# Moving the squares of queries and keys from GpSimd to ScalarE in a fused decoder's first self-attention

## Chip, cores and metric

The kernel runs on one core of a Trainium2 chip, as one launch. The metric is device time in microseconds (us); lower is better. TensorE is called PE here, its weight loads PEld, VectorE DVE, ScalarE ACT and GpSimd POOL.

## What is computed

Two decoder layers on x of shape (16, 128, 256), float32. Each layer is a self-attention, a cross-attention and a feed-forward part, each followed by a residual addition and a layer norm. The change is in the first part of layer 0, which treats the 16 batch entries as 16 separate tiles of 128 tokens with 16 heads of 128:

```
q  = rope(rmsnorm(x @ Wq  + bq,  qn_w))        # rmsnorm: t * rsqrt(mean(t*t) + eps) * w
lk = rope(rmsnorm(x @ Wlk + blk, kn_w))
lv = x @ Wlv + blv
ck, cv = keys and values of 32 compressed entries (weighted sums of 4 tokens)
sparse = softmax over the 8 largest of q.ck, times cv
local  = softmax(causal q.lk), times lv
x = layernorm(x + ((sparse + local) / 2) @ Wo + bo)
```

The mean of squares of every head of q and lk is what the changed instructions feed.

## The kernel before, in words

`l0_attention` gives each engine its own program. The programs meet only through semaphores. A `Count` is a semaphore with a fixed number of increments in each tile; `of(b, k)` is its value after the k-th of tile b, and `before(c, b, k, n)` the value n increments ahead of that.

The order of the work is written out by hand: the list `order` names pieces with a lag, and `pipeline` emits on every engine, in that order, the pieces which that engine has. In pass i a piece with lag 0 works on tile i, one with lag 1 on tile i-1. So a pass mixes the projections of tile i with the attention of tile i-1. Passes 0 and 1 are emitted apart, passes 2 to 15 are a loop, and two passes drain it. The list holds

```
... ("s1", 1), ("norm1", 2), ("q", 0), ("sparse_exp", 1), ("sparse_prob", 1), ("rot_q", 0), ("norm2", 2),
("e0", 1), ("k", 0), ("e1", 1), ("turn_sparse", 1), ("m0", 1), ("sum_q", 0), ("top2", 1), ("entries", 0), ("m1", 1) ...
```

What each engine does in the pieces that matter here:

- Piece `q`, and likewise `k`: PE projects 4 chunks of 512 columns (L452, L454) into two PSUM banks in turn; ACT copies each chunk to `raw` (L605); before the change POOL then squares the whole 128x2048 of it into `sq` (L388). There is one `sq` tile for both. So the keys' square waits until DVE has summed the queries' (`summed`, L387).
- Piece `rot_q` (DVE): rotary embedding of the raw queries, L702 to L707. Piece `sum_q` (DVE): sums of squares of each head, L748, and a scale, L749; the keys have `rot_k` and `sum_k`.
- Pieces `sum_q`, `k_norm`, `comp_kv` on POOL: the powers -1/2 (L394, L399, L408), and the scaling of the rotated keys (L403).
- Pieces `e0` and `e1` (ACT): exponentials of the local scores of head groups 0 and 1, L645, with the bias `a_nbias` from DVE (L793, L795). `sparse_exp` (ACT, L636) and `sparse_prob` (DVE, L776 to L783) are the sparse softmax; `turn_sparse` is its transposition (PE, L525) and copy (ACT, L654).
- Pieces `m0` to `m3`, one for each head group: DVE normalises the probabilities (L804, L805), PE transposes them (L547), ACT copies that out (L660), PE multiplies by the values (L561, L562), ACT copies (L666), PE applies Wo (L535). In `m0` PE also makes the scores of group 2 and ACT their exponentials. Piece `entries` lies between `m0` and `m1`: PE L438, ACT L592.

Each engine works strictly through its own list, so an instruction that waits holds all that stands behind it.

Of the kernel before, what the change touches and what calls it, by code (L numbers as in the profile page):

```python
# [10 lines left out]
ALU = mybir.AluOpType  # L11
ACT = mybir.ActivationFunctionType
# [68 lines left out]
def pipeline(eng, order, pieces, passes):  # L81


    depth = max(lag for _, lag in order)

    def emit(i, there):
        for name, lag in order:
            if name in pieces and there(lag):
                pieces[name](i - lag)

    for i in range(depth):
        emit(i, lambda lag, i=i: lag <= i)
    with eng.Fori(depth, passes) as i:  # L93
        emit(i, lambda lag: True)
    for i in range(passes, passes + depth):
        emit(i, lambda lag, i=i: i - lag < passes)
# [18 lines left out]
def bcast(ap, shape):  # L115

    return ap.unsqueeze(2).to_broadcast(shape)
# [133 lines left out]
def l0_attention(core, wcol, weights):  # L251
    nc, A = core.nc, core.A
    NG = NH // G
    w_qkv, w_o, w_c = weights.qkv, weights.o, weights.c
    with ExitStack() as ctx:
        def sb(name, shape, dt=F32):
            return ctx.enter_context(nc.sbuf_tensor(name, shape, dt))
# [9 lines left out]
        def count(name, per):  # L267
            return Count(sem(name), per)
# [10 lines left out]
        raw = [sb(f"a0_raw{n}", [P, NH * D]) for n in "qkv"]  # L279
        rot = [sb(f"a0_rot{n}", [P, NH * D]) for n in "qk"]  # L280
        sq = sb("a0_sq", [P, NH * D])
# [45 lines left out]
        tile_in = count("tile_in", 1)  # L327
# [3 lines left out]
        Q_AT, K_AT, C_AT, V_AT = 1, 5, 9, 10  # L331
        proj_made, proj_read = count("proj_made", PROJ), count("proj_read", PROJ)

        work_made, work_read = count("work_made", 3 * NG), count("work_read", 2 * NG)
        squared, summed, rotated = count("squared", 2), count("summed", 2), count("rotated", 2)
        root_h, k_normed, rqs_up = count("root_heads", 2), count("k_normed", 1), count("rqs_up", 1)
        wsel_up, c_sum, root_c, crot_up = (count(n, 1) for n in ("wsel_up", "c_sum", "root_c", "crot_up"))
        c_made = count("c_made", 4)
        c_read = count("c_read", 3)
        s_arg, s_exp, s_prob = (count("sparse_" + n, 1) for n in ("arg", "exp", "prob"))  # L340
        bias_up, l_exp, l_prob = (count(n, NG) for n in ("bias_up", "local_exp", "local_prob"))
        pT_made, pT_read = count("pT_made", NG), count("pT_read", NG)
        cT_made, cT_read = count("cT_made", NG), count("cT_read", NG)
        o_made, o_read = count("o_made", 1), count("o_read", 1)
        var_up, root_l, x_up = count("var_up", 1), count("root_l", 1), count("x_up", 1)

        def before(c, b, k, n):

            return c.of(b, k - n) if k > n else c.of(b - 1, c.per + k - n)
# [3 lines left out]
        order = [("turn_q", 1), ("sparse", 1), ("turn_k", 1), ("in", 0), ("s0", 1), ("s1", 1), ("norm1", 2),  # L353
# [3 lines left out]
                 ("k_norm", 0), ("comp_kv", 0), ("v", 0), ("comp_key", 0)]  # L357
# [3 lines left out]
        @block.sync  # L361
        def _(sp):
            for j, name in enumerate(("L0_attn_qn_w", "L0_attn_kn_w")):
                sp.dma_start(wn[:, j, :], A[name].partition_broadcast(P)).then_inc(loaded, 16)
            for t, name in ((cq, "c_cos"), (ck_tab, "c_cos"), (cc, "c_cos_c"), (sq_tab, "c_sin"),
                            (sk_tab, "c_sin"), (sc_tab, "c_sin_c"), (cmask_f, "c_cmask"), (member, "c_member")):
                sp.dma_start(t[:, :], A[name]).then_inc(loaded, 16)
            sp.wait_ge(loaded, 16 * LOADS)
            sp.wait_ge(weights.loaded, weights.all_in)

        @block.gpsimd
        def _(pool):
            for c in (tile_in, squared, root_h, k_normed, root_c, root_l):
                c.open(pool)

            def tile_copy(b):


                pool.wait_ge(proj_made.sem, proj_made.of(b - 1, 1))
                pool.wait_ge(c_made.sem, c_made.of(b - 1, 1))  # L380
                pool.tensor_copy(xb[:, :], core.x[:, bass.ds(b, 1), :].rearrange("p o h -> p (o h)")).then_inc(tile_in.sem, 1)

            def square(j):
                def run(b):

                    pool.wait_ge(proj_read.sem, proj_read.of(b, (Q_AT, K_AT)[j] + 4))
                    pool.wait_ge(summed.sem, before(summed, b, j + 1, 1))  # L387
                    pool.tensor_tensor(sq[:, :], raw[j][:, :], raw[j][:, :], ALU.mult).then_inc(squared.sem, 1)  # L388
                return run

            def root_queries(b):
                pool.wait_ge(summed.sem, summed.of(b, 1))
                pool.wait_ge(rqs_up.sem, rqs_up.of(b - 1))
                pool.tensor_tensor(rstd[:, 0:NH], ssq[:, 0:NH], core.neghalf[:, 0:NH], ALU.pow).then_inc(root_h.sem, 1)  # L394

            def norm_keys(b):
                pool.wait_ge(summed.sem, summed.of(b, 2))
                pool.wait_ge(k_normed.sem, k_normed.of(b - 1))
                pool.tensor_tensor(rstd[:, NH:], ssq[:, NH:], core.neghalf[:, 0:NH], ALU.pow).then_inc(root_h.sem, 1)  # L399
                pool.wait_ge(root_h.sem, root_h.of(b, 2))  # L400
                pool.wait_ge(rotated.sem, rotated.of(b, 2))
                kr = rot[1][:, :].rearrange("p (h d) -> p h d", h=NH)
                pool.tensor_tensor(kr, kr, bcast(rstd[:, NH:], [P, NH, D]), ALU.mult).then_inc(k_normed.sem, 1)  # L403

            def root_compressed(b):
                pool.wait_ge(c_sum.sem, c_sum.of(b))
                pool.wait_ge(crot_up.sem, crot_up.of(b - 1))
                pool.tensor_tensor(cst[:, 2:3], cst[:, 1:2], core.neghalf[:, 0:1], ALU.pow).then_inc(root_c.sem, 1)  # L408

            def root_layer(b):  # L410
                pool.wait_ge(var_up.sem, var_up.of(b))
                pool.wait_ge(x_up.sem, x_up.of(b - 1))
                pool.tensor_tensor(ln_r[:, :], mv[:, 1:2], core.neghalf[:, 0:1], ALU.pow).then_inc(root_l.sem, 1)

            pipeline(pool, order, {"in": tile_copy, "q": square(0), "k": square(1), "norm1": root_layer,
                                   "sum_q": root_queries, "k_norm": norm_keys, "comp_kv": root_compressed}, B)

        @block.tensor
# [156 lines left out]

        @block.scalar
        def _(act):
            for c in (work_read, proj_read, c_read, s_exp, l_exp, pT_read, cT_read):
                c.open(act)
            act.wait_ge(tables, TABLES)  # L580

# [13 lines left out]
            def projected(i, at):  # L595
                def run(b):

                    if i < 2:
                        act.wait_ge(rotated.sem, rotated.of(b - 1, i + 1))
                        act.wait_ge(squared.sem, squared.of(b - 1, i + 1))  # L600
                    else:
                        act.wait_ge(cT_made.sem, cT_made.of(b - 1))
                    for c in range(NG):
                        act.wait_ge(proj_made.sem, proj_made.of(b, at + c + 1))
                        act.copy(raw[i][:, c * BANK:(c + 1) * BANK], proj[(at + c) % 2][:, :]).then_inc(proj_read.sem, 1)  # L605
                return run

            def compressed_up(b):
# [47 lines left out]
            def group(g):  # L656
                def run(b):
# [6 lines left out]
                    if g == 0:  # L664
                        act.wait_ge(o_made.sem, o_made.of(b - 1))
                    act.copy(cT[g % 2][:, :, :].rearrange("p g t -> p (g t)"), p_cT[:, :]).then_inc(cT_read.sem, 1)  # L666
                return run

            pieces = {"turn_q": heads_up(0), "turn_k": heads_up(1), "in": inputs_up, "q": projected(0, Q_AT),
                      "k": projected(1, K_AT), "sparse_exp": sparse_exp, "e0": exps(0), "e1": exps(1),  # L670
                      "turn_sparse": sparse_up, "entries": entries_up, "comp_kv": compressed_up,
                      "v": projected(2, V_AT), "comp_key": compressed_key_up}
            pieces.update({f"m{g}": group(g) for g in range(NG)})
            pipeline(act, order, pieces, B)
# [1591 lines left out]
```

## Time and profile before

| | before |
|---|---|
| median of 3 runs | 4181.91 us (4170.14 to 4184.75) |
| profiled execution, first to last instruction | 4173.1 us; the profile gives no device time of its own for it |
| median less that span | 8.8 us |
| PE busy | 3568.3 us, 86% of the span |
| DVE busy | 2268.4 us, 54% |
| ACT busy | 1854.3 us, 44% |
| POOL busy | 567.6 us, 14% |
| mean granted TensorE clock | 0.894 of 2.4 GHz |

Times in the trace count from the first instruction. The self-attention of layer 0 ends at about 1180 us. A timeline row has the start in us, the time taken in us, the engine, the line, the operation, the tile written and the tiles read, and in brackets how long the engine had been idle before it and who released it. A line of waits has the waiting engine, tile and line, the releasing one, and then the sum in us, the number of times and the longest in us. "x_res", "a_sq" and so on are the program's tile names without the `0` of the layer.

### The profile page before, as it was taken

What the parts mean: (1) busy time and instruction counts of PE and PEld (TensorE: products, weight loads), DVE (VectorE), ACT (ScalarE), POOL (GpSimd) and SP (SyncE); (2) the same over time, 40 slices, a digit from 0 to 9 for tenths busy, and PEclk for the clock granted to TensorE, in tenths of its full rate; (3) what the DMA queues carried; (4) which work ended last, traced back from release to release, by engine and by line L of the source; (5) the groups of instructions that cost most, each with busy time, mean ns of one, the idle gap of its engine ahead of it and who ended that gap; (6) DMA issues with size and microseconds to landing.
All of it is one profiled execution on the core that took longest, in us unless ns stands there. A gap on an engine that the chain in (4) does not pass through costs nothing. (4 is left out here: it accounts for less than half of the span.)

```text
span 4173.1 us, 66457 instructions
## 1 busy us (share of the span) xinstructions
PE 3568.3 (86%) x20492; PEld 2302.4 (55%) x20492; DVE 2268.4 (54%) x4684; ACT 1854.3 (44%) x3823; POOL 567.6 (14%) x326
## 2 busy tenths in 40 slices
PE   4899989898856688888888887989996888999998
PEld 2565656565643455555555553557774555555554
DVE  4645454546438877777777774225552544232222
ACT  1433333333325888888888881124442333111110
POOL 1222222222230000000000001013331222000000
PEclk9999999999978988888888885989997988999999
DMA  3000000000000000000000001000003000000000
GB/s 111 1 0 0 0 0 0 0 0 0 0 16 13 0 0 0 0 0 0 0 0 0 0 0 33 0 10 0 0 0 118 7 6 4 1 0 0 0 0 20
DMA packets 33662, 35.55 MB, mean 9 GB/s; under 512 B 2925, under 2 KB 32081, under 8 KB 32849
## 3 DMA queue, kind: packets, MB, share of 16 engines
q10 hardware_dynamic: 17360, 19.22, 1.4%
q1 hardware_dynamic: 16256, 15.77, 1.2%
q8 instruction: 24, 0.39, 0.0%
q14 instruction: 22, 0.17, 0.0%
HBM read 32.83 MB, written 2.10 MB: 8 GB/s over the span
## 5 line engine op out<-in xcount | busy, mean ns | idle before, releaser
L1301 ACT ACTIVATE x_ints<-x_p_s,x_nb,x_sq 128x512 uint16<-128x512 f32 (+1 forms) x768 | 697.7, 916 | 103.6 <-DVE x_nb L1330 103.0
L1318 DVE TENSOR_REDUCE x_hmax<-x_p_s 128x1 f32<-128x1024 f32 x512 | 626.5, 1224 | 89.8 <-PE x_p_s L1213 51.9
L1213 PE MATMUL x_p_s<-x_kT,x_qz 128*128 (+1 forms) x1024 | 409.6, 465 | 152.6 <-ACT x_ints L1301 140.2
L1238 PE MATMUL x_p_t<-identb,x_ints 128*128 128x128 bf16 x4096 | 384.6, 249 | 48.0 <-DVE x_turned L1337 26.7
L2083 DVE TENSOR_TENSOR f_h<-f_act_g,f_p_u 128x512 f32<-128x512 f32 (+1 forms) x132 | 90.7, 687 | 548.9 <-PE f_p_y L1978 480.5
L1238 PEld LDWEIGHTS x_p_t<-identb,x_ints 128*128 128x128 bf16 x4096 | 292.9, 111 | 135.0 <-issue 75.6
L1247 PEld LDWEIGHTS x_p_o<-x_vi,x_turned 128*128 128x128 bf16 x4096 | 260.8, 100 | 140.6 <-issue 69.1
L2028 ACT ACTIVATE f_act_g<-f_p_g 128x512 f32<-128x512 f32 (+1 forms) x132 | 78.4, 597 | 577.6 <-PE f_p_g L1963 577.5
L1247 PE MATMUL x_p_o<-x_vi,x_turned 128*128 (+1 forms) x4096 | 309.3, 176 | 0.9 <-DVE x_att L1343 0.9
L1293 ACT CAST x_turned<-x_p_t 128x1024 bf16<-128x1024 uint16 x256 | 259.1, 1012 | 112.7 <-PE x_p_t L1238 112.6
L1963 PE MATMUL f_p_g<-f_xT,f_wg 128*128 128x512 f32 (+1 forms) x528 | 271.1, 638 | 15.4 <-ACT f_xT L2015 10.2
L1963 PE MATMUL f_p_u<-f_xT,f_wu 128*128 128x512 f32 (+1 forms) x528 | 252.4, 601 | 0.0
L1978 PE MATMUL f_p_y<-f_wd,f_h 128*128 128x256 f32 (+1 forms) x1056 | 247.9, 379 | 0.0
L1978 PEld LDWEIGHTS f_p_y<-f_wd,f_h 128*128 128x128 f32 (+1 forms) x1056 | 200.3, 190 | 77.6 <-issue 56.5
L1213 PEld LDWEIGHTS x_p_s<-x_kT,x_qz 128*128 (+1 forms) x1024 | 96.8, 111 | 260.0 <-issue 134.3
L1337 DVE CAST x_turned<-x_p_t 128x1024 bf16<-128x1024 uint16 x256 | 176.0, 688 | 87.9 <-PE x_p_t L1238 83.2
L1787 DVE TENSOR_REDUCE s_rmax<-s_p_s 128x4 f32<-128x512 f32 x128 | 88.4, 691 | 177.6 <-PE s_p_s L1637 176.6
L1395 POOL TENSOR_TENSOR x_ln_r<-x_mv,neghalf 128x1 f32<-128x1 f32 x16 | 8.7, 542 | 1262.2 <-DVE x_mv L924 1262.2
L1963 PEld LDWEIGHTS f_p_u<-f_xT,f_wu 128*128 128x128 f32 (+1 forms) x528 | 102.8, 195 | 133.1 <-issue 127.6
L1649 PEld LDWEIGHTS s_p_o<-s_vaug,s_eT 128*128 128x128 f32 x1024 | 132.2, 194 | 56.5 <-issue 38.3
L1963 PEld LDWEIGHTS f_p_g<-f_xT,f_wg 128*128 128x128 f32 (+1 forms) x528 | 95.4, 196 | 112.4 <-issue 92.9
L1301 ACT ACTIVATION_READ_ACCUMULATOR x_ints<-x_p_s,x_nb,x_sq (+1 forms) x768 | 151.2, 197 | 0.0
(334 smaller groups left out, 6273.0 us busy)
## 6 DMA issues: line engine op xcount, KB each, us to landing
f_wg<-in_L_ffn_w_dram ACTq DMA_DIRECT2D x2, 1408.0 KB, 9.0
f_wu<-in_L_ffn_w_dram ACTq DMA_DIRECT2D x2, 1408.0 KB, 9.9
f_wd<-in_L_ffn_w_dram ACTq DMA_DIRECT2D x1, 2816.0 KB, 10.9
x_res<-in_x_dram SPq DMA_DIRECT2D x1, 2048.0 KB, 8.3
a_wq<-in_L_attn_Wq_dram ACTq DMA_DIRECT2D x1, 2048.0 KB, 7.6
a_wk<-in_L_attn_Wlk_dram ACTq DMA_DIRECT2D x1, 2048.0 KB, 12.0
a_wv<-in_L_attn_Wlv_dram ACTq DMA_DIRECT2D x1, 2048.0 KB, 16.3
a_wo<-in_L_attn_Wo_dram ACTq DMA_DIRECT2D x1, 2048.0 KB, 21.5
```

The lines of the kernel that those rows point to most:

```text
L1213: return pe.matmul(p_s[half][par][:, c * BANK:(c + 1) * BANK], qz[:, par, :, :, :].rearrange("p a b t -> p (a b) t")[:, bass.ds(n, 1), :]. ...
L1238: mm = pe.transpose(p_t[:, c * P:(c + 1) * P], ints[par][:, half, c * P:(c + 1) * P].bitcast(BF16), core.identb[:, :])
L1247: mm = pe.matmul(p_o[:, 0:XD], turned[par][:, k, :], vi[:, k, bass.ds(a * (2 * XD) + par * XD, XD)], start=(k == 0), stop=(k == B - 1))
L1293: act.copy(turned[par][:, 8:16, :].rearrange("p k n -> p (k n)"), p_t[:, :].bitcast(U16)).then_inc(t_act.sem, 1)
L1301: act.activation(ints[par][:, half, lo:hi], p_s[half][par][:, lo:hi], ACT.Exp, bias=nb[:, par:par + 1], scale=of_pass(sq[:, par, :, :].rea ...
L1318: dve.tensor_reduce(hmax[:, par, half:half + 1], p_s[half][par][:, :], AX.X, ALU.max).then_inc(max_up.sem, 1)
L1337: dve.tensor_copy(turned[par][:, 0:8, :].rearrange("p k n -> p (k n)"), p_t[:, :].bitcast(U16)).then_inc(t_dve.sem, 1)
L1649: mm = pe.matmul(p_o[:, n * (dk + 1):(n + 1) * (dk + 1)], eT[g % 2][:, h, :], vaug[:, n, :], start=(n == 0), stop=(n == heads - 1))
L1787: mid.link(dve.tensor_reduce(top, s3, AX.X, ALU.max))
L1963: mm = pe.matmul(bank[n % 2][0:m, :], w[:, t, n * P:n * P + m], xT[:, t, :], start=(t == 0), stop=(t == KT - 1))
L1978: mm = pe.matmul(p_y[j // 2][:, (j % 2) * H:(j % 2 + 1) * H], h[n % 2][0:m, j * P:(j + 1) * P], wd[0:m, n, :], start=(n == 0 and j % 2 == ...
L2083: i = dve.tensor_tensor(h[n % 2][0:m, :], act_g[n % 2][0:m, :], p_u[n % 2][0:m, :], ALU.mult)
```

## The change

POOL loses the two pieces that square; ACT gets a 128x2048 `Square` at the end of its pieces `q` and `k`, behind its four copies and the same two waits. Nothing else moves, and there is still one `sq` tile.

```diff
@@ @block.gpsimd
-            for c in (tile_in, squared, root_h, k_normed, root_c, root_l):
+            for c in (tile_in, root_h, k_normed, root_c, root_l):
-            def square(j):
-                def run(b):
-
-                    pool.wait_ge(proj_read.sem, proj_read.of(b, (Q_AT, K_AT)[j] + 4))
-                    pool.wait_ge(summed.sem, before(summed, b, j + 1, 1))
-                    pool.tensor_tensor(sq[:, :], raw[j][:, :], raw[j][:, :], ALU.mult).then_inc(squared.sem, 1)
-                return run
-            pipeline(pool, order, {"in": tile_copy, "q": square(0), "k": square(1), "norm1": root_layer,
+            pipeline(pool, order, {"in": tile_copy, "norm1": root_layer,
@@ @block.scalar
-            for c in (work_read, proj_read, c_read, s_exp, l_exp, pT_read, cT_read):
+            for c in (work_read, proj_read, c_read, s_exp, l_exp, pT_read, cT_read, squared):
@@ def projected(i, at):
                     for c in range(NG):
                         act.wait_ge(proj_made.sem, proj_made.of(b, at + c + 1))
                         act.copy(raw[i][:, c * BANK:(c + 1) * BANK], proj[(at + c) % 2][:, :]).then_inc(proj_read.sem, 1)
+                    if i < 2:
+
+                        act.wait_ge(proj_read.sem, proj_read.of(b, at + NG))
+                        act.wait_ge(summed.sem, before(summed, b, i + 1, 1))
+                        act.activation(sq[:, :], raw[i][:, :], ACT.Square).then_inc(squared.sem, 1)
```

For the queries (i = 0) the second wait is for the key sums of the tile before; for the keys (i = 1) it is for the query sums of the same tile.

How this moves instructions shows best on ACT, in the loop's pass, from the last copy of the raw keys to the copy of the transposed probabilities of group 0. What each waits for stands in brackets. Before:

```order
L605 COPY a_rawk<-a_p_proj 128x512 [waits a0_proj_made]
L640 REGISTER_ALU
L645 ACTIVATE a_prob,a_lsum<-a_p_work,a_nbias,a_rqs 128x128 [waits a0_pT_made,a0_local_prob,a0_bias_up]
L645 ACTIVATE a_prob,a_lsum<-a_p_work,a_nbias,a_rqs 128x128 x3
L652 REGISTER_ALU
L654 COPY a_psT<-a_p_c 128x512 [waits a0_cT_made,a0_c_made]
L660 COPY a_pT<-a_p_pT 128x512 [waits a0_cT_made,a0_pT_made]
```

The same place with the change (its line numbers are a few lower):

```order
L597 COPY a_rawk<-a_p_proj 128x512 [waits a0_proj_made]
L601 ISA [waits a0_proj_read]
L602 ACTIVATE a_sq<-a_rawk 128x2048 [waits a0_summed]
L637 REGISTER_ALU
L642 ACTIVATE a_prob,a_lsum<-a_p_work,a_nbias,a_rqs 128x128 [waits a0_pT_made,a0_local_prob,a0_bias_up]
L642 ACTIVATE a_prob,a_lsum<-a_p_work,a_nbias,a_rqs 128x128 x3
L649 REGISTER_ALU
L651 COPY a_psT<-a_p_c 128x512 [waits a0_cT_made,a0_c_made]
L657 COPY a_pT<-a_p_pT 128x512 [waits a0_cT_made,a0_pT_made]
```

The square of the keys, with its wait for the query sums, now stands ahead of the exponentials of group 1 and of both copies.

On POOL, one pass before:

```order
L388 TENSOR_TENSOR a_sq<-a_rawq 128x2048
L388 TENSOR_TENSOR a_sq<-a_rawk 128x2048
L394 TENSOR_TENSOR a_rstd<-a_ssq,neghalf 128x16
L399 TENSOR_TENSOR a_rstd<-a_ssq,neghalf 128x16
L403 TENSOR_TENSOR a_rotk<-a_rotk,a_rstd 128x2048
L408 TENSOR_TENSOR a_cst<-a_cst,neghalf 128x1
```

and with the change:

```order
L386 TENSOR_TENSOR a_rstd<-a_ssq,neghalf 128x16
L391 TENSOR_TENSOR a_rstd<-a_ssq,neghalf 128x16
L395 TENSOR_TENSOR a_rotk<-a_rotk,a_rstd 128x2048
L400 TENSOR_TENSOR a_cst<-a_cst,neghalf 128x1
```

The two squares are gone from POOL and the rest keeps its order.

## Rows read from the trace of the kernel before

**Rows 1.** Waits of PE in the first self-attention, from 84 to 1180 us.
```profile
PE a_p_pT L547 <- DVE a_prob L805: 68.2, 28, 3.5
```

**Rows 2.** Timeline of ACT in one pass of the loop.
```profile
530.85 0.59 ACT L605 COPY a_rawq<-a_p_proj 128x512 f32<-128x512 f32 x1 [1.65 <-PE a_p_proj L454]
531.33 0.63 ACT L636 ACTIVATE a_es<-a_scm 128x512 f32<-128x512 f32 x1
...
533.60 0.60 ACT L605 COPY a_rawk<-a_p_proj 128x512 f32<-128x512 f32 x1
...
539.77 0.59 ACT L605 COPY a_rawk<-a_p_proj 128x512 f32<-128x512 f32 x1 [1.65 <-PE a_p_proj L454]
540.25 0.46 ACT L645 ACTIVATE a_prob<-a_p_work,a_nbias,a_rqs 128x128 f32<-128x128 f32 x1
...
542.01 0.60 ACT L654 COPY a_psT<-a_p_c 128x512 f32<-128x512 f32 x1
544.31 0.59 ACT L660 COPY a_pT<-a_p_pT 128x512 f32<-128x512 f32 x1 [1.71 <-PE a_p_pT L547]
```

**Rows 3.** Timeline of PE in the same pass.
```profile
543.62 0.65 PE L547 MATMUL a_p_pT<-ident,a_prob 128*128 128x128 f32 x4 [3.45 <-DVE a_prob L805]
...
545.22 0.39 PE L561 MATMUL a_p_cT<-a_pT,a_rawv 128*128 128x128 f32 x2
...
547.00 0.53 PE L438 MATMUL a_p_c<-a_wsel,a_xb 128*128 128x32 f32 x4
...
550.47 0.66 PE L547 MATMUL a_p_pT<-ident,a_prob 128*128 128x128 f32 x4 [2.93 <-DVE a_prob L805]
```

**Rows 4.** Timeline of DVE and POOL in the same pass.
```profile
532.00 3.75 DVE L776 SCALAR_TENSOR_TENSOR a_es<-a_repl,a_es 128x512 f32<-128x512 f32 x1 [6.27 <-ACT a_es L636]
...
542.80 0.69 DVE L805 SCALAR_TENSOR_TENSOR a_prob<-a_prob,a_lrec 128x512 f32<-128x512 f32 x1
...
545.72 0.17 DVE L749 TENSOR_SCALAR a_ssq<-a_ssq 128x16 f32<-128x16 f32 x1
...
545.98 3.60 POOL L388 TENSOR_TENSOR a_sq<-a_rawk 128x2048 f32<-128x2048 f32 x1 [10.77 <-DVE a_ssq L749]
...
546.55 3.05 DVE L795 SCALAR_TENSOR_TENSOR a_nbias<-a_lmax,a_rqs 128x4 f32<-128x4 f32 x1
```

**Rows 5.** Timeline of DVE in the last tile, where POOL squares nothing.
```profile
1162.29 0.68 DVE L776 SCALAR_TENSOR_TENSOR a_es<-a_repl,a_es 128x512 f32<-128x512 f32 x1
```

**Rows 6.** Groups of ACT by shape: count, busy us, mean ns, idle before.
```profile
L1301 ACT ACTIVATE x_ints<-x_p_s,x_nb,x_sq 128x512 uint16<-128x512 f32 x512 | 393.9, 773 | 103.6 <-DVE x_nb L1330 103.0 <-issue 0.2
L1301 ACT ACTIVATE x_ints<-x_p_s,x_nb,x_sq 128x1024 uint16<-128x1024 f32 x256 | 307.2, 1200 | 0.0
```

**Rows 7.** Timeline of PE in two other passes, where it restarts for group 0.
```profile
262.04 1.02 PE L547 MATMUL a_p_pT<-ident,a_prob 128*128 128x128 f32 x4 [3.45 <-DVE a_prob L805]
...
614.94 1.11 PE L547 MATMUL a_p_pT<-ident,a_prob 128*128 128x128 f32 x4 [3.45 <-DVE a_prob L805]
```

**Rows 8.** Windows of PE there: stretch, length, busy (instructions), granted clock, DMA, GB/s.
```profile
264.00:266.00 2.00, 2.00 (x13) 0.60 0.00 0
...
619.00:621.00 2.00, 2.00 (x13) 0.61 0.00 0
```

**Rows 9.** Timeline of pass 0: DVE, ACT, POOL, PE.
```profile
60.72 1.28 DVE L704 TENSOR_TENSOR a_half<-a_rawq,a_sin_q 128x512 f32<-128x512 f32 x2
...
65.59 2.29 DVE L702 TENSOR_TENSOR a_rotk<-a_rawk,a_cos_k 128x2048 f32<-128x2048 f32 x1
67.81 4.71 DVE L704 TENSOR_TENSOR a_half<-a_rawk,a_sin_k 128x512 f32<-128x512 f32 x2
...
63.30 0.59 ACT L605 COPY a_rawk<-a_p_proj 128x512 f32<-128x512 f32 x1 [1.64 <-PE a_p_proj L454]
...
76.26 2.97 POOL L399 TENSOR_TENSOR a_rstd<-a_ssq,neghalf 128x16 f32<-128x16 f32 x1 [1.60 <-DVE a_ssq L749]
...
83.91 0.48 PE L474 MATMUL a_p_c<-ident,a_crot 128*128 128x128 f32 x1 [9.23 <-DVE a_crot L725]
```

## The prediction

> **What bounds the kernel now.** The page comes first, as the table above gives it: PE is busy 86% of the span and POOL 14%, so POOL's own time is no bound. Then the waits of the first self-attention: what PE waits for is DVE's normalised probabilities, 68.2 us in 28 waits [rows 1]. Last, the timeline of one pass, engine by engine [rows 2 to 4]. The pass shown has the widest waits of PE.
>
> In it PE stands still twice: 3.45 us until DVE has the probabilities of group 0 at 543.49 (542.80 + 0.69), and 2.93 us until it has those of group 1 [rows 3, 4]. Behind both lie POOL's squares. While POOL squares the queries, L776 on DVE takes 3.75 us; in the last tile, with no square beside it, 0.68 [rows 4, 5]. While POOL squares the keys, from 545.98 to 549.58, L795 takes 3.05 us for 4 columns a partition and ends with the square, at 549.60 [rows 4]. Group 1 can be normalised only then, since it stands behind L795 on DVE. So PE's start at 550.47 is set by POOL. POOL's square of the keys in turn has stood 10.77 us idle for the sums of the queries [rows 4]. That idle time costs nothing on POOL, but the change takes the wait along to ACT.
>
> **What a square costs on ACT.** No such instruction is in the trace. ACT's exponential of 512 columns takes 773 ns and of 1024 columns 1200 [rows 6]: 427 ns for 512 more, 0.834 ns a column. The 128x512 exponential from SBUF takes 0.63 us [rows 2], which gives 0.63 + 1536 x 0.834 ns = 1.91 us for 2048. The lower bound is 1.71, the slope alone; the upper bound is POOL's 3.60 for the same work [rows 4]. I take 1.91, being nearest in engine and type.
>
> **Queries.** The last raw copy ends at 531.44 [rows 2]. The square runs from 531.5 to 533.4, and the sparse exponential behind it starts at 533.3 instead of 531.33, 1.97 later. The raw keys' copies come 1.97 later too, the first from 535.57 to 536.16. PE's third key chunk needs that bank, so two more chunks are made from 536.2 on, 2.24 us each (the 1.65 of idle and 0.59 of copy [rows 2]), and the last key copy starts at 540.7 instead of 539.77 and ends at 541.4. This 1 us of PE lies ahead of its first idle stretch, which shrinks by it, so it costs nothing; without that stretch it would be 1 us a pass. On DVE, L776 starts 1.97 later and lasts 3.07 less [rows 4, 5]. What follows it there has no gaps, so the probabilities of group 0 are ready at 543.49 - 1.1 = 542.4 and the sums of the queries at 545.89 - 1.1 = 544.8. PE's first wait ends 1.1 us earlier.
>
> **Keys.** ACT has copied the keys at 541.4 but must wait for those sums until 544.8. The square ends at 546.8. Behind it in ACT's list stand the exponentials of group 1, 1.76 us to the start of L654 (540.25 to 542.01 [rows 2]), then L654 and, about 0.5 behind it, L660. So they start at 546.7, 548.5 and 548.95, and L660 ends at 549.55 instead of 544.90. PE waits for that. It goes from L547 to the end of the group 2 scores in 1.6 us [rows 3], so it is through at 544.1 and stands still until 549.6, some 5.4 us. Before, it did the value products and the entries from 545.22 to 547.53 [rows 3], ahead of its wait. Now they come after it: 549.6 + 2.31 = 551.9 for the transposes of group 1, against 550.47. DVE has group 1 ready at 549.5 and is no bound, with L795 no longer held. From there the pass keeps its spacing. That is **1.4 us a pass**. Passes 1 to 15 hold both a square and an attention: 15 x 1.4 = 21 us.
>
> **The clock.** After PE's first idle stretch the granted clock falls from the upper of its two levels, 2.4 GHz, to the lower, 1.2, in most passes. PE restarts at 262.0 in one and 614.9 in another [rows 7]. In the first the clock averages 0.60 at 264 to 266, so it is low until about 265.6, 3.5 us after the restart. In the second it is 0.61 at 619 to 621, low until about 620.6, 5.7 us after [rows 8]. Before, this cost nothing: the slow work lay ahead of the second wait. With the change the long idle stretch comes last, the work behind it has no wait left to hide in, and 5.4 us is longer than the 3.45 that already brings the fall. The fall comes earlier against the restart, since the stall is some 2 us longer. So 1.5 to 5.7 us at half speed, half of it lost: 0.8 to 2.9 us. I take the middle, 1.9, which is **15 x 1.9 = 28 us**.
>
> The Trainium skill, "TensorE: Matmul & The Clock Gate", section "HAM oscillation — how this bites in real kernels", speaks against the change here: a long enough wait of PE in every turn of a loop throttles it afresh each turn, and the price is paid each time, not once. By that rule the sum has this term in every pass; without it the sum is that of the waits alone. The low clock behind the shorter stalls agrees with it.
>
> **Pass 0.** Nothing is overlapped here. The raw keys are copied at 63.89 [rows 9], and DVE, whose rotation of the queries is over by then without a square beside it, can start on them at 63.95 instead of 65.59. From there to the start of POOL's L399 it took 76.26 - 65.59 = 10.67 us, with 4.71 us in L704 where the same pair takes 1.28 with POOL idle [rows 9]; so 7.24 now, and L399 starts at 71.2. From L399 to PE's L474 it was 83.91 - 76.26 = 7.65 us [rows 9], so PE goes on at 78.85, **5 us earlier**. The keys' square delays ACT's entry copies and PE's value projections by 2 us, inside PE's 9.23 us of idleness [rows 9]. I count nothing for the clock there.
>
> **Sum.** 21 + 28 - 5 = +44 us on the 4173.1 of the profiled span. The median lies 8.8 us above that span, so on it 4181.9 + 44 = **4226 us**.
>
> **The rivals.**
> 1. The clock stays high behind the new stall. For it: the pass of [rows 3] transposes group 0 in 0.65 us, against 1.02 and 1.11 [rows 7], behind the same 3.45. Against: 5.4 us is longer. Then 21 - 5 = +16, 4198 us.
> 2. The wait for the sums does not hold ACT, and the kernel gets faster. It decides at the end of `sum_q` on DVE: if that comes before the last key copy ends (541.4; I have 544.8), square, exponentials and copies run through, L660 ends at 546.1, and group 1 is transposed from 546.2 + 2.31 = 548.5 instead of 550.47. That is 2.0 x 15 = 30, with pass 0 35 us less: 4147. For it: DVE gets 3.07 and nearly 3 us a pass back. Against: `sum_q` stands behind the rotation and group 0 on DVE, 3.4 us too late. The Trainium skill, "GPSIMD Engine Reference", section "4.1 Engine selection", sends elementwise work of two inputs away from GpSimd as about twice as slow; taken as a rule it would side with this rival. The trace's 3.60 against my estimate of 1.91 agrees on the instruction, not on its place.
> 3. The square costs on ACT what it costs on POOL, 3.60 [rows 4]. Both squares lie in the chain, so 2 x 1.7 x 15 = 51 more: 4277.
> 4. The change is empty: what the added wait costs, the contention that is gone gives back, within some 8 us.
>
> **Chances.** The forecast with wait and clock 0.55 (its own range, by the bounds of the clock, 4210 to 4241); rival 1 0.25; rival 2 0.08; rival 3 0.05; rival 4 0.07. A measurement of this kernel can tell about 0.5%, 21 us, from no change; the three runs shown differ by 14.6. Slower by more: nearly all of the forecast, rival 3, and 0.3 of rival 1, whose value lies just below the line: 0.66. Within: 0.25. Faster: 0.09. The range 4180 to 4256 takes in rival 1 less the spread of the runs, the upper half of rival 4, and the forecast's upper bound plus that spread; it leaves out rivals 2 and 3.
>
> **What would show it.** Right: a square of about 1.9 us on ACT; ACT idle some 3.4 us ahead of the keys' square, for DVE's sums; L776 (now L773) at 0.68 us, L795 (now L792) no longer held; PE idle 5 us ahead of the first L561 (now L553), for ACT's L660 (now L657), and hardly ahead of the second L547 (now L539); the clock low behind it; PE's L474 (now L466) first at about 79 us. Wrong: no such wait on ACT (rival 2), a high clock through the stall (rival 1), a square over 2.5 us (rival 3).

## The result, and the profile after

The changed kernel takes **4206.0 us** (median of four runs, 4201.03 to 4213.9) against 4178.27 us of the kernel before (four runs, 4170.14 to 4184.75). The ratio is 1.007, with a 95% interval of 1.0051 to 1.0088: slower by 0.7%, some 28 us. The forecast was 4226 us in a range of 4180 to 4256, with slower by over 0.5% as the likeliest case.

Below are waits of the first self-attention in the kernel after. Each line has the engine, tile and line, what it waited for, and then the us in total, the number of times and the longest.

```profile
PE a_p_cT L553 <- ACT a_pT L657: 79.7, 15, 5.4
PE a_p_pT L539 <- DVE a_prob L802: 19.8, 15, 1.4
PE a_p_proj L444 <- ACT a_rawk L597: 14.7, 15, 1.0
```

```profile
ACT a_sq L602 <- DVE a_ssq L746: 51.8, 15, 3.5
```

PE's wait for DVE's probabilities was 68.2 us in 28 waits [rows 1]. It is now 19.8 us in 15. PE now waits first of all for ACT's copy of the transposed probabilities, 5.3 us in each of 15 passes, and 1.0 for the third key copy. Ahead of that stands a wait that was not there before: ACT, 3.5 us in each pass, for DVE to read the queries' squares out of `sq`.

Next comes the timeline of ACT in one pass of the kernel after. It answers to [rows 2].

```profile
616.17 0.58 ACT L597 COPY a_rawq<-a_p_proj 128x512 f32<-128x512 f32 x1 [1.65 <-PE a_p_proj L446]
616.86 1.91 ACT L602 ACTIVATE a_sq<-a_rawq 128x2048 f32<-128x2048 f32 x1
618.68 0.61 ACT L633 ACTIVATE a_es<-a_scm 128x512 f32<-128x512 f32 x1
...
626.15 0.58 ACT L597 COPY a_rawk<-a_p_proj 128x512 f32<-128x512 f32 x1 [1.65 <-PE a_p_proj L446]
...
630.21 1.91 ACT L602 ACTIVATE a_sq<-a_rawk 128x2048 f32<-128x2048 f32 x1 [3.47 <-DVE a_ssq L746]
...
633.76 0.59 ACT L651 COPY a_psT<-a_p_c 128x512 f32<-128x512 f32 x1
634.22 0.61 ACT L657 COPY a_pT<-a_p_pT 128x512 f32<-128x512 f32 x1
```

DVE in the same pass:

```profile
619.33 0.69 DVE L773 SCALAR_TENSOR_TENSOR a_es<-a_repl,a_es 128x512 f32<-128x512 f32 x1 [8.35 <-ACT a_es L633]
...
630.00 0.17 DVE L746 TENSOR_SCALAR a_ssq<-a_ssq 128x16 f32<-128x16 f32 x1
630.82 0.16 DVE L792 SCALAR_TENSOR_TENSOR a_nbias<-a_lmax,a_rqs 128x4 f32<-128x4 f32 x1
```

L773, once L776, takes 0.69 us where it took 3.75. L792, once L795, takes 0.16 where it took 3.05 and ended with POOL's square [rows 4]. DVE is freed as intended. But the sums end at 630.17, ACT's square of the keys starts right behind them, and everything after it in ACT's list is late.

PE in the same pass, answering to [rows 3], and the windows from its restart on (stretch, length, busy us and instructions, granted clock, DMA, GB/s):

```profile
627.90 0.65 PE L539 MATMUL a_p_pT<-ident,a_prob 128*128 128x128 f32 x4 [1.35 <-DVE a_prob L802]
...
634.96 0.79 PE L553 MATMUL a_p_cT<-a_pT,a_rawv 128*128 128x128 f32 x2 [5.31 <-ACT a_pT L657]
...
638.55 0.63 PE L539 MATMUL a_p_pT<-ident,a_prob 128*128 128x128 f32 x4
```

```profile
635.00:637.00 2.00, 2.00 (x9) 0.50 0.00 0
637.00:639.00 2.00, 2.00 (x17) 0.80 0.00 0
```

PE has no wait left ahead of the second L539. It stands still before L553 and goes on at half clock: 0.50 of full speed is the lower level, 1.2 GHz. From L553 to the second L539 it takes 3.59 us in this pass. In [rows 3] the same work took 547.53 - 545.22 = 2.31, at full clock, as the windows of the kernel before show:

```profile
544.00:546.00 2.00, 2.00 (x19) 1.00 0.00 0
546.00:548.00 2.00, 1.54 (x15) 1.00 0.00 0
```

**Where the time went.** A pass, from one to the next start of DVE's copy L758 (L761 before), was 70.63 us on average over passes 1 to 15. It is 73.38 now. The traces of both kernels show three parts of the difference. The first is the wait. From the last raw query copy to the transposes of group 1 it was 19.62 us. In this pass it is 638.55 - 616.17 = 22.38; less the 3.59 - 2.31 = 1.28 of the clock, that leaves 21.10, a wait that grew by 1.5 us. The second is the clock. The stretch from L553 to the second L539 takes 4.28 us in every second pass instead of 3.6; over all fifteen it has a mean of 3.96, and the clock costs 3.96 - 2.31 = 1.65. Wait and clock together are 3.1. The third part gives 0.4 back, since the entry scores run less at the low clock. Here is their group in the first self-attention, before and after (line, engine, operation, tiles, form and count; busy us and mean ns of one; idle before):

```profile
L501 PE MATMUL a_p_c<-a_ckT,a_qT 128*128 128x32 f32 x512 | 73.4, 309 | 0.0
```

```profile
L493 PE MATMUL a_p_c<-a_ckT,a_qT 128*128 128x32 f32 x500 | 66.6, 296 | 0.0
```

32 of them a pass by 13 ns are 0.4 us. So 2.75 x 15 = +41 us, and the copy that starts pass 1 comes 5.9 us earlier. At the end of the stage +35 should stand, and it does. This is the first group of the stage that follows, before and after (count, least, median and greatest ns, first and last start):

```profile
L1024 POOL COPY x_xb<-x_res x16: 398/532/582, 1220.4 to 1306.2; 128x256 f32 x16
```

```profile
L1021 POOL COPY x_xb<-x_res x16: 396/532/573, 1255.5 to 1340.8; 128x256 f32 x16
```

From 1220.4 to 1255.5 is +35.1. The span grew by 26.1 only (4173.1 to 4199.2): the rest of the kernel took 2943.7 us after and 2952.7 before. The experiments below show that this rest, which the change doesn't touch, varies by as much from run to run.

The granted clock is 0.93 on average over the passes of both kernels, before and after:

```profile
93.20:1152.70 1059.50, 951.97 (x4352) 0.93 0.00 0
```

```profile
87.30:1187.90 1100.60, 947.46 (x4351) 0.93 0.00 0
```

So the change did not make the clock low for a larger share of a pass. It moved a fall. Before, PE ran slowly behind its wait for group 0 in most passes, and the wait for group 1 took that up: the transposes of group 1 came 19.6 us behind the last query copy in all passes but the first, whether the clock was low or not. After the change nothing behind the slow stretch takes it up.

### The profile page after: what moved, and what is told of

The parts are those of the page before. It is cut to its first block and busy times, and to the rows that moved or that the text cites. A ratio compares the mean times of both kernels' runs of the same rounds, so it can differ in the third digit from the quotient of the medians.

```text
span 4199.2 us, 66429 instructions
## 1 busy us (share of the span) xinstructions
PE 3548.4 (85%) x20492; PEld 2287.3 (54%) x20492; DVE 2186.7 (52%) x4684; ACT 1912.0 (46%) x3855; POOL 450.3 (11%) x294
## 5 line engine op out<-in xcount | busy, mean ns | idle before, releaser
L553 PE MATMUL a_p_cT<-a_pT,a_rawv 128*128 128x128 f32 x512 | 114.9, 311 | 79.7 <-ACT a_pT L657 79.7
```

The source lines that it names most:

```text
L553: pe.matmul(o, raw[2][:, at:at + D], pT[g % 2][:, h, :], start=(h == 0), stop=False)
```

## The experiments

The experiments ask four things: whether the low clock behind the stall carries its part, whether the wait for the sums is what hurts, which of the two squares costs and which gains, and whether another place for the same squares is faster. "Pass" below is always the mean of passes 1 to 15, read from DVE's copy of the entry scores. All diffs but those of the third and fourth experiment are against the changed kernel.

### PE kept busy in the stall

```diff
 # PE, group(g), behind the scores of group 2
+                    if g == 0:
+                        pe.wait_ge(cT_read.sem, cT_read.of(b, 0))
+                        for _ in range(FILL):          # 20
+                            pe.matmul(p_cT[:, :], core.identb[:, :], core.causal[...], start=True, stop=True)
```

The products that follow overwrite what these 20 bf16 products of 512 columns leave in the bank.

> The changed kernel, with 20 bf16 matmuls of 512 columns (identity by causal mask, their result overwritten) put on PE between the group 2 scores and the value products of group 0, that is into its 5.3 us wait for ACT. They compute nothing that is used. Theory (wait plus clock): the wait is ACT's, so PE restarts at the same place, but now at the full clock, and from the first L553's restart to the second L539 it takes 2.3 us instead of 3.6 to 4.3 (mean 3.96). That is 1.65 us a pass, 15 passes: about 25 us less than the changed kernel, 4181 us, and 15 x 1.4 - 6 = +15 us or a little less against before. Rival (the clock costs nothing there, PE's slow work is hidden): as the changed kernel, 4206 us. Rival (the matmuls are in the way): slower than 4206.

Measured: 4181.24 us (ten runs, 4176.93 to 4191.23) against 4174.55, ratio 1.002 (1.0009 to 1.0031). PE in this kernel, and its windows:

```profile
613.39 4.48 PE L547 MATMUL a_p_cT<-causal,identb 128*128 128x512 bf16 x20
...
618.86 0.48 PE L559 MATMUL a_p_cT<-a_pT,a_rawv 128*128 128x128 f32 x2 [0.99 <-ACT a_pT L663]
...
621.11 0.63 PE L540 MATMUL a_p_pT<-ident,a_prob 128*128 128x128 f32 x4
```

```profile
618.00:620.00 2.00, 1.14 (x10) 1.00 0.00 0
620.00:622.00 2.00, 2.00 (x20) 1.00 0.00 0
```

The stall is as long as before (4.48 us of filling and 0.99 of idleness), ACT's wait is the same 51.8 us in 15, and the clock is 1.00 in both windows. The stretch from L559 to L540 takes 2.25 us instead of 3.96. A pass is 71.08 us instead of 73.38, so 2.3 shorter: 1.7 of it lies right behind the stall, and the other 0.6 is spread over the pass, where the clock also stays high more of the time.

That is 2.3 x 15 = 34.5 us in the passes, and yet the profiled spans differ by 23.2 and the medians by 25. In the last tile nothing is squared, PE has no such stall, and the filling is simply in the way:

```profile
1169.96 4.79 PE L547 MATMUL a_p_cT<-causal,identb 128*128 128x512 bf16 x20
1174.58 0.38 PE L559 MATMUL a_p_cT<-a_pT,a_rawv 128*128 128x128 f32 x2
```

There the filled kernel loses 4.4 us, and the rest of the kernel took 6.8 us longer in this execution. **With the clock held high the fifteen passes are 34.5 us shorter, some 25 of them right behind the stall.** That the medians differ by just the 25 us expected is in part luck. Against before, the passes of the filled kernel are 0.45 x 15 = 6.8 us longer, pass 0 is 6.0 shorter and the last tile 4.2 longer, 5.0 in all; the medians say 6.7.

### The sums of the queries ahead of their rotation

```diff
-                 ... ("sparse_prob", 1), ("rot_q", 0), ("norm2", 2), ("e0", 1), ("k", 0),
-                 ("e1", 1), ("turn_sparse", 1), ("m0", 1), ("sum_q", 0), ("top2", 1), ...
+                 ... ("sparse_prob", 1), ("sum_q", 0), ("rot_q", 0), ("norm2", 2), ("e0", 1), ("k", 0),
+                 ("e1", 1), ("turn_sparse", 1), ("m0", 1), ("top2", 1), ...
 # and the counts of DVE's chain of rotations and sums in their new order
```

> The changed kernel, with DVE's sums of the query squares placed ahead of the rotation of the queries instead of behind group 0. ACT then finds them done when it has copied the keys. Theory (the wait for the sums on ACT's list is what costs): ACT's wait ahead of the keys' square goes from 3.5 us to nothing, PE restarts for the value products of group 0 some 3.4 us earlier, and the transposes of group 1 come about 2.0 us earlier in the pass than before the change; the stall of PE falls to about 2 us and the clock fall with it. 30 to 35 us less over the passes, 6 in pass 0: about 4140 us. Rival (it is ACT's added 3.8 us of work a pass that costs, wherever it waits): as the changed kernel, 4206 us.

Measured: ten runs in two groups, four at 4130.5 to 4139.36 and six at 4177.24 to 4192.48 us; median 4179.88, ratio 0.9979 (0.994 to 1.0018), unclear. In the traces of both groups ACT's wait for the sums is gone, and so is PE's stall at L553, although the keys' square still stands where the change put it. But PE waits for group 0 again, and longer. The sums stand on DVE ahead of it, and POOL's power of the queries now runs beside DVE's rotation. From the trace of one of the four shorter runs:

```profile
525.76 1.11 PE L539 MATMUL a_p_pT<-ident,a_prob 128*128 128x128 f32 x4 [3.97 <-DVE a_prob L802]
...
L386 POOL TENSOR_TENSOR a_rstd<-a_ssq,neghalf x16: 4908/5095/5097, 59.6 to 1065.9; 128x16 f32<-128x16 f32 x16
```

The expectation did not count the sums' own 2.4 us on the way to group 0. Why one kernel has two times was unknown at this point. The same kernel was executed twice more for its trace, with an idea stated ahead: that the transposes of the keys fall into the low clock in one pattern of passes and not in the other.

> The kernel of e2 once more, for its profile: its executions lay at 4130 to 4139 us and at 4177 to 4192. Theory (PE's clock): the passes fall into one of two patterns that repeat from pass to pass; in the long one the granted clock is low twice a pass, as before the change, and a pass takes some 3 us more than the 68.27 of the short one. Rival (something outside this stage differs): passes of 68.27 again at whatever total time.

> The kernel of e2 a third time, for its profile, in the hope of the longer of its two patterns (4177 to 4192 us). Theory: then the granted clock is low in the keys' transposes as well as behind PE's stall, and a pass takes some 71.3 us instead of 68.27. Rival: passes of 68.27, and the difference lies in another stage.

The first of the two took 4139.6 us, with passes of 67.57 to 68.50 us, and of 68.27 or 68.28 from the sixth to the fourteenth. The other took 4179.27 us, with passes of 70.64 to 72.29, mean 71.73. In the same place of a pass, this kernel's short run and then the long one:

```profile
561.72 3.65 PE L493 MATMUL a_p_c<-a_ckT,a_qT 128*128 128x32 f32 x32
565.21 1.07 PE L482 MATMUL a_p_work<-ident,a_rotk 128*128 128x128 f32 x8
```

```profile
513.77 4.72 PE L493 MATMUL a_p_c<-a_ckT,a_qT 128*128 128x32 f32 x32
518.30 3.74 PE L482 MATMUL a_p_work<-ident,a_rotk 128*128 128x128 f32 x16
```

```profile
513.00:518.00 5.00, 4.46 (x32) 0.81 0.00 0
518.00:522.00 4.00, 4.00 (x20) 0.50 0.00 0
```

In the long run the 32 entry scores take 1.1 us longer and the transposes run at 0.50 throughout; in the short run this place has a clock of 1.00. The fall behind the wait for group 0 differs as well, in the short run and then the long one:

```profile
525.00:529.00 4.00, 3.24 (x16) 0.57 0.00 0
```

```profile
546.00:554.00 8.00, 5.49 (x26) 0.57 0.00 0
```

A mean of 0.57 means 3.4 us at half clock in the 4.00 of the short run, and 6.9 in the 8.00 of the long one. PE waits for group 0 equally long in both, 59.0 us in 15. So this variant could not price the wait for the sums: the later group 0 and the two patterns of the clock lie on top of it.

### One square alone

```diff
 # third experiment: POOL keeps the square of the keys
+                    if i == 0:
+                        ...
+                        act.activation(sq[:, :], raw[i][:, :], ACT.Square).then_inc(squared.sem, 1)
 # fourth experiment: POOL keeps the square of the queries
+                    if i == 1:
```

> Only the queries are squared on ACT; the keys' square is on POOL, as before. Theory: L776 is no longer held (-3.07) but starts 1.97 later, so the whole middle of the pass comes 1.1 us earlier: POOL's keys' square ends at 548.5 instead of 549.6 of the pass shown, and with it the bias of group 1. PE's last stall stays short. 15 x 1.1 = 16 us less, 2 in pass 0: about 4160 us, faster than before. Rival (ACT's added work costs): slower than before by half of the change, about 4192 us.

> Only the keys are squared on ACT; the queries' square is on POOL, as before. Theory: L776 is held for 3.75 us again, so the sums end at 545.9, ACT squares the keys to 547.9, and the copy L657 ends at 550.65; PE's group 1 comes at 553.0 instead of 550.47, 2.5 us later, plus 1.65 for the clock: 15 x 4.2 = 63 us more, 3 less in pass 0: about 4238 us, the slowest of the four. Rival (ACT's added work costs): slower by half of the change, about 4192 us, as for the queries alone.

Queries alone: 4170.17 us (ten runs), ratio 0.9991 (0.998 to 1.0001), no difference. Keys alone: 4245.28 us (four runs, 4231.21 to 4246.16), ratio **1.0169** (1.0152 to 1.0186). PE's waits of the first and of the second, and what ACT waits for in the second:

```profile
PE a_p_pT L547 <- DVE a_prob L810: 60.4, 30, 2.7
```

```profile
PE a_p_cT L561 <- ACT a_pT L665: 62.4, 15, 4.2
PE a_p_pT L547 <- DVE a_prob L810: 51.2, 15, 3.5
```

```profile
ACT a_sq L610 <- DVE a_ssq L754: 83.2, 15, 5.6
```

The loss comes with the keys' square. Alone it costs more than both together, for it holds ACT for 5.5 us a pass, since DVE, still slowed by POOL's square of the queries, has the sums even later. The queries' square does on ACT what was forecast of it. Group 0 waits 1.35 us instead of 3.45, of which 1.0 moved to the third key chunk, so the probabilities come 1.1 earlier. But DVE's biases (L800) still end with POOL's square of the keys, at the second wait. The 1.1 us x 15 = 16 us did not reach the time: a pass is 70.47 against 70.63. The clock in the later part of the pass is what took them, as the trace has it. Here are two stretches from group 1 to the next group 0, of 64.6 and 60.6 us. PE is idle for about as long in both, 4.8 and 5.3 us, and the clock differs:

```profile
127.50:192.10 64.60, 59.78 (x257) 0.92 0.00 1
199.00:259.60 60.60, 55.31 (x258) 1.00 0.00 0
```

From group 1 to the end of the pass it is 36.4 us on average against 35.6 before, so 0.9 of the 1.1 is lost there. No run with the clock held high isolates it.

### The squares at a later place on ACT

The square becomes a piece of its own with the same two waits, and the table of the order says where it stands. In the fifth and sixth experiment the queries' square stays right behind `q`, as in the change.

```diff
+            def squared_up(i, at):
+                def run(b):
+                    act.wait_ge(proj_read.sem, proj_read.of(b, at + NG))
+                    act.wait_ge(summed.sem, before(summed, b, i + 1, 1))
+                    act.activation(sq[:, :], raw[i][:, :], ACT.Square).then_inc(squared.sem, 1)
+                return run
 # keys behind group 1 (fifth), behind group 3 (sixth); queries behind the exponentials of group 0 as well (seventh)
-                 ("entries", 0), ("m1", 1), ...
+                 ("entries", 0), ("m1", 1), ("sq_k", 0), ...
-                 ("m2", 1), ("m3", 1), ("sum_k", 0), ...
+                 ("m2", 1), ("m3", 1), ("sq_k", 0), ("sum_k", 0), ...
-                 ("e0", 1), ("k", 0),
+                 ("e0", 1), ("sq_q", 0), ("k", 0),
```

> The changed kernel, with the square of the keys in its own piece on ACT behind the piece of group 1 (m1), so no longer ahead of the exponentials of group 1 and the copies of the sparse and group 0 probabilities. The squares' work on ACT is the same. Theory (place in ACT's list, not work): no stall of 5.3 us ahead of the first L553; PE transposes group 1 some 3.8 us earlier in the pass than before the change; the square then holds the copy of group 2 by 1.3 us and costs PE 0.6 to 0.8. So some 3 us a pass less than before the change, and 6 in pass 0: about 4125 us. Rival (ACT's added 3.8 us of work a pass costs anywhere): 4206 us.

> As e5, but with the keys' square behind group 3 (m3), into ACT's idle 3.35 us ahead of the compressed keys. Theory: the gain of 3.8 us stays whole, but DVE's sums of the keys now end at about 570.2 of the pass shown, and POOL's chain of power, scaling and power behind them lets PE's L466 start 0.5 to 1 us late: 3 us a pass less than before the change, 6 and less in pass 0, since there this chain sets the end: about 4130 us. Rival (ACT's work): 4206 us.

> As e6 (keys' square behind group 3), and the square of the queries moved too, behind the exponentials of group 0. Theory: the sparse exponential and DVE's chain behind it are no longer 1.97 us late, so the 1.35 us that PE still waits for group 0 in e6 goes; the third key chunk still waits 1 us for its bank. Some 1.2 us a pass less than e6, 18 in all: about 4091 us, if the clock pattern does not give it back. Rival (the queries' square costs only where it delays the key copies, and that is unchanged): as e6, 4109 us.

> The kernel before, once more, for its profile. The changed kernel's first self-attention ends 35.1 us later in its profile, but its span is only 26.1 us longer, though nothing behind that stage differs. Theory (the stages behind vary from execution to execution with the clock): here the time from the end of the first self-attention to the end of the span differs from that of the first profile by several us. Rival (the change speeds up what follows): it agrees within 1 us.

| kernel | median us (runs) | ratio to before (95%) | pass us |
|---|---|---|---|
| before | 4178.27 (4) | | 70.63 |
| keys behind group 1 | 4116.46 (4) | 0.9862 (0.9841 to 0.9883) | 66.73 |
| keys behind group 3 | 4108.78 (4) | 0.9848 (0.9825 to 0.9872) | 66.76 |
| and queries behind the exponentials | **4102.42** (5) | **0.9827** (0.9813 to 0.984) | 66.25 |
| before, executed once more | 4175.7 (1) | | 70.59 |

Each ratio is against runs of before on the same chip, with medians of 4178.58 us for the first two and 4172.48 for the third. PE's waits with the keys' square behind group 3, and then with both squares later:

```profile
PE a_p_pT L539 <- DVE a_prob L806: 19.9, 15, 1.4
PE a_p_proj L444 <- ACT a_rawk L597: 14.7, 15, 1.0
```

```profile
PE a_p_cT L553 <- ACT a_pT L660: 22.5, 15, 1.5
PE a_p_proj L444 <- ACT a_rawk L597: 11.7, 15, 0.8
```

The squares are the same instructions on the same engine as in the change. The keys' square, with its 3.5 us of wait for the sums and its own 1.9 us of work, no longer stands ahead of group 1, and 28 us of loss become 70 us of gain. In the pass of [rows 3], the waits of before, 3.45 and 2.93, give way to 1.35 and 1.0; that is 4.0. In the other passes before, slow work took the place of part of the 2.93; over all fifteen, the time from the last query copy to the transposes of group 1 goes from 19.6 us to 15.7, and the pass is 3.9 shorter. The fifth and the sixth came out faster than expected, by 9 and 21 us, mostly because the costs expected further down the pass hardly came: there the keys' square makes PE wait 0.3 us a pass in the fifth and nothing in the sixth. Between the fifth and the sixth the pass does not differ. In the seventh the wait for group 0 is gone, but the next limit is close: ACT's exponentials of group 1 stand behind the last key copy, which goes by PE's projections, and PE waits 1.5 us for the copy behind them. So it gains 0.5 us a pass of the 1.35, and its median is 4102 where 4091 was expected. It has the lowest median of this study. It is clearly faster than the kernel before and the changed one; its interval overlaps that of the sixth, and only the pass in the trace tells these two apart.

A second `sq` tile for the keys would take the wait away in the place of the change. It was not tried, so how the loss divides between the wait for the sums and the square's own 1.9 us is read from ACT's timeline and not from a run.

## Why the prediction was right, step by step

**The square on ACT**, 1.91 us from two exponentials of other lengths [rows 6], is 1.91 us in all 32 cases. Rival 3, at 3.60, falls.

**Queries.** L773 at 0.69, the wait of 1.0 for the third key chunk, and group 0 some 1.1 us earlier are all there. That this gains nothing by itself, as the third experiment has it with a ratio of 0.9991, I had not foreseen: I had expected 4160 us of that kernel.

**Keys.** The wait of ACT for the sums was forecast at 3.4 us and is 3.5, the stall of PE at 5.4 and is 5.3. From the start of the queries' square to PE's restart 549.6 - 531.5 = 18.1 us were forecast, and 634.96 - 616.86 = 18.1 are measured. The term of 1.4 us a pass measures 1.5. The third and fourth experiment find the loss with this square and none with the other, and the moved squares take it away.

**The clock** was the larger term: 1.9 us a pass in bounds of 0.8 to 2.9. It measures 1.65 behind the stall. By the total alone rival 1, a high clock at 4198 us, was nearer to the measured 4206 than the forecast of 4226. The windows at 0.50 decide against it, and so does the first experiment: with the clock held high in the same stall a pass is 2.3 us shorter, 1.7 of them right behind the stall. The Trainium skill, "TensorE: Matmul & The Clock Gate", section "HAM oscillation — how this bites in real kernels", has the price paid anew in every turn of a loop, and the trace agrees: the windows show 0.50 behind the stall in this pass, and the stretch is about 3.6 or 4.28 us in all fifteen, never 2.31.

**Pass 0** was forecast 5 us shorter, with the rotated entries' transpose (L466) at 78.85. The row agrees:

```profile
79.02 0.33 PE L466 MATMUL a_p_c<-ident,a_crot 128*128 128x128 f32 x1 [0.63 <-DVE a_crot L722]
```

By the start of pass 1 the gain is 5.9 us. One execution says little of its size: in the second one of the kernel before, L474 starts at 84.90 instead of 83.91, and pass 1 starts 3.7 us later.

**The sum** was 44 us; the medians show 28 and the two profiled spans 26. Between 44 and 26 lie 18 us. The clock term was too large by 0.25 x 15 = 4. The 0.4 us a pass that came back in the entry scores, 6 us, was not in the sum. Pass 0 gave 1 more, and the wait cost 1 more. The other 9 us of the profiled span lie in the rest of the kernel, which no step of the sum touches. Span minus the start of that rest is 2952.7 us before, 2949.5 in the second trace of the same kernel, 2943.7 after, and between 2944.0 and 2955.2 in the experiments. Three traces of one kernel, that of the second experiment, have 2949.4, 2955.2 and 2945.3. That much one profiled execution can be off, in either direction. Only the wait erred in the other direction, by 1 us, so the forecast is not right through terms that cancel.

**Rival 2**, the wait not holding ACT, was right about what lies behind it and wrong that this change reaches it. Its condition, the sums ready when the last key copy ends, was missed by 3.5 us. When the table of the order takes the square out of the way, the kernel gets faster by 70 us and not by the 35 that the rival gave: 3.9 us a pass instead of 2.0. The rival still had the square's own 1.9 us ahead of group 1, and those are gone too. The Trainium skill, "GPSIMD Engine Reference", section "4.1 Engine selection", which sends elementwise work of two inputs away from GpSimd, names VectorE as the engine to take; here the squares went to ScalarE. Leaving GpSimd agrees with the seventh experiment's kernel, by 1.7%, and not with this change: the rule says nothing of the place in the new engine's list.

**Rival 4**, no change within 8 us, falls by the interval: 1.0051 to 1.0088 of 4178 us is 21 to 37 us. **Rival 1** is answered above under the clock.

## What to carry to other kernels

A piece that moves to another engine brings its waits along, and there they hold whatever stands behind it in program order; the same two squares cost 0.7% right behind the copies and gain 1.7% further down the list. Place such a piece by the time when its last wait ends, not by the time when its data is there. And price a stall of PE in a loop twice, once as the wait and once as the stretch at half clock behind it, when no other wait is left to hide that stretch: here the second was slightly the larger, 1.65 us a pass against 1.5.

## What the runs showed of the hardware that I had not expected

- One kernel, with the same wait of PE for group 0 in every pass, has two times 1.2% apart, 4130.5 to 4139 and 4177 to 4192 us, and the traces differ in the granted clock. In the shorter pattern it is low once a pass, for 3.4 us; in the longer one twice, for some 6.8 us each time. In the shorter pattern the passes settle to 68.27 us, within 0.01 of it from the sixth to the fourteenth. A median over few runs of such a kernel says little.
- The clock can fall without a long idle stretch of PE ahead. In the longer pattern it falls inside the run of 32 float32 products of 32 columns (3.65 us at full clock, 4.72 with the fall in them), with PE busy for 4.46 of 5.00 us, and the longest idle stretch of PE in the 30 us before is the 0.75 us just ahead of them:

```profile
513.54 0.39 PE L490 MATMUL a_p_c<-a_cmask,identb 128*128 128x512 bf16 x1 [0.75 <-ACT a_qT L626]
```

- POOL's power on 16 columns takes 2.9 us in the changed kernel and 5.1 us beside DVE's rotation. Moving the squares away did not end the contention of the two engines: another order of DVE's list brought it back, on POOL's side.
- Useless products in a stall of PE bought 25 us back, nearly all that the change had lost; where there was no stall to fill, in the last tile, they cost 4.4 us.
